# A recommendation tower on one core: one-hots compared against row numbers in PSUM, eight picked tables, strips in single runs, another order on PE, and filler products

## What is computed

```python
e = jnp.stack([tbl_f[ids[:, f]] for f in range(26)], axis=1)     # 512 x 26 x 128
sd = jnp.einsum('bfd,bd->bf', e, dense)
ss = jnp.einsum('bfd,bgd->bfg', e, e)
z = jnp.concatenate([dense, sd, ss[:, iu, ju]], axis=1)           # iu, ju: the pairs above the diagonal
h = jnp.concatenate([z, dense], axis=1)                           # 512 x 607
h = jnp.maximum(h @ W_top1 + b_top1, 0.0)                         # 512
h = jnp.maximum(h @ W_top2 + b_top2, 0.0)                         # 256
y = h @ W_top3                                                    # 512 x 1
```

## Time and profile before

| | |
|---|---|
| median of three runs | 146.29 us |
| the profiled execution | 145.72 us, of which the span (first to last instruction) 143.9 us |
| PE busy | 108.4 us (75%) |
| DVE busy | 65.0 us (45%) |
| ACT busy | 61.4 us (43%) |
| POOL busy | 82.6 us (57%) |
| DMA | 14.86 MB, 8258 packets, 4629 of them under 512 bytes |

### The profile page before, as it was taken

The page is one execution under the profiler, slowest core; times in us unless marked ns, Lnnn a source line. Parts: engine busy times, 40 slices in busy tenths (PEclk is TensorE's granted clock), DMA queues, the critical chain, the costliest instruction groups (busy, mean ns, idle before and its releaser), DMA issues.

```text
span 143.9 us, 1888 instructions
## 1 busy us (share of the span) xinstructions
PE 108.4 (75%) x692; PEld 97.4 (68%) x692; DVE 65.0 (45%) x138; ACT 61.4 (43%) x101; POOL 82.6 (57%) x76
## 2 busy tenths in 40 slices
PE   0007999999999999859509999979950989960792
PEld 0006778887887879758409997879940979950782
DVE  3079759999999934242400544215430013320011
ACT  4205077758997949818401245643320112320011
POOL 4788878998889977777777777777710000000000
PEclk9999999999999999999955999999997579996599
DMA  4999926999893342222232222321121000002000
GB/s 83 338 248 273 305 54 175 315 280 268 223 255 105 91 114 59 55 55 50 66 85 55 59 55 66 85 70 44 50 53 38 0 5 0 0 1 44 10 0 1
DMA packets 8258, 14.86 MB, mean 103 GB/s; under 512 B 4629, under 2 KB 4629, under 8 KB 8250
## 3 DMA queue, kind: packets, MB, share of 16 engines
q1 hardware_dynamic: 5805, 10.21, 25.5%
q0 software_dynamic: 2176, 4.46, 12.3%
q10 hardware_dynamic: 269, 0.09, 0.3%
HBM read 13.96 MB, written 0.00 MB: 97 GB/s over the span
## 4 chain that ended last, share of the span: by engine, by line
POOL 33%; PE 28%; SPq 13%; DMA 10%; issue 9%; DVE 3%; ACTq 2%; ACT 0%
POOL rows L289 33%; SPq L227 13%; PE ps_h_bank L368 12%; PE ps_gram L347 11%; DMA dots<-hot_ids 3%; DMA dots<-table 3%; ACTq L686 2%; DMA rows<-in_tbl,ids_sb 2%; PE ps_h_bank L388 1%; PE ps_dve L330 1%; DMA ids_sb<-in_ids 1%; DVE table L532 1%; DVE hot_ids L532 1%; PE ps_act L330 1%; PE ps_h_bank L400 1%
## 5 line engine op out<-in xcount | busy, mean ns | idle before, releaser
L289 POOL DMA_INDIRECT rows<-in_tbl,ids_sb x68 | 81.8, 1202 | 21.7 <-issue 20.4
L347 PE MATMUL ps_gram<-vecs 128*128 128x108 f32 x256 | 30.7, 276 | 1.1 <-issue 0.9
L498 DVE TENSOR_SCALAR one_hot<-hot_ids,row_id 125x512 fp32r<-125x512 int32 x67 | 27.9, 491 | 7.8 <-DMA hot_ids<-in_hot_ids 6.0
L302 PE MATMUL ps_gram<-one_hot,table_hi 125*128 125x512 f32 x78 | 31.2, 419 | 0.0
L347 PEld LDWEIGHTS ps_gram<-vecs 128*128 128x128 f32 x256 | 29.6, 192 | 1.9 <-issue 1.9
L302 PE MATMUL ps_gram<-one_hot,table_lo 125*128 125x512 f32 x78 | 30.6, 412 | 0.0
L368 PE MATMUL ps_h_bank<-dots,w_dots 128*128 128x128 f32 x96 | 17.6, 359 | 16.8 <-DMA dots<-hot_ids 10.0
L368 PEld LDWEIGHTS ps_h_bank<-dots,w_dots 128*128 128x128 f32 x96 | 16.4, 267 | 17.5 <-DMA dots<-table 7.2
L302 PEld LDWEIGHTS ps_gram<-one_hot,table_lo 125*128 125x128 f32 x78 | 15.5, 199 | 3.9
L302 PEld LDWEIGHTS ps_gram<-one_hot,table_hi 125*128 125x128 f32 x78 | 15.2, 200 | 3.4
L489 DVE COPY vecs<-ps_dve 128x512 f32<-128x512 f32 (+1 forms) x10 | 9.2, 923 | 14.9 <-PE ps_dve L330 14.9
(11 more groups left out here) (36 smaller groups left out, 83.6 us busy)
## 6 DMA issues: line engine op xcount, KB each, us to landing
table<-in_tbl SPq DMA_DIRECT2D x6, 448.0 KB
hot_ids<-in_hot_ids SPq DMA_DIRECT2D x3, 768.0 KB, 5.1
table<-in_tbl SPq DMA_DIRECT2D x3, 560.0 KB
rows<-in_tbl,ids_sb POOLq DMA_INDIRECT x68, 2.6
w_dots<-in_w_dots SPq DMA_DIRECT2D x3, 256.0 KB, 3.5
w_dense<-in_w_dense SPq DMA_DIRECT2D x2, 256.0 KB, 5.8
w<-in_W_top SPq DMA_DIRECT2D x2, 256.0 KB, 2.9
table<-in_tbl SPq DMA_DIRECT2D x6, 52.0 KB
```

The costliest lines, as they stand in the source:

```text
L289: pool.indirect_dma_start(out=rows[:, t % ROW_SETS, k, :], out_offset=None, in_=ins[f"tbl_{f}"], in_offset=bass.IndirectOffsetOnAxis(ap=id ...
L302: return pe.matmul(ps_pick[:, i % 2, :], part[0:KP, i % PART_RING, k, :], one_hot[0:KP, i % HOT_RING, k, :], start=(part is table_hi and k ...
L347: last = pe.matmul(ps_gram[:, part % 2 * BANKS + g // PER_BANK, c0:c0 + COLS], vecs[:, t % 2, p0:p0 + QUADS, :], vecs[:, t % 2, p0:p0 + QU ...
L498: nc.vector.tensor_scalar(one_hot[0:KP, i % HOT_RING, k, :], hot_ids[0:KP, i, :], row_id[0:KP, at + k:at + k + 1], None, ALU.is_equal).the ...
```

## The change

- `HOT` loses table 8 (1250 rows); eight tables are picked, 18 are gathered (72 gathers; the last batch of a tile has two tables).
- The row numbers are copied once to PSUM (`ps_row_id`). DVE makes the one-hots of two steps in one `tensor_tensor` of 125x1024, ids from SBUF and row numbers from PSUM, both read with step 0 along one dimension. ACT makes the last two steps of every table, table 0 included. DVE makes 6 of 8, or 8 of 10.
- ids are loaded as one table's, three and four tables' (`IDS_GROUPS`); the biases and `W_top3` are loaded later.
- `sums` is laid out so that each row's part of a strip is one run of 1536 bytes, and `gram` puts its four blocks of a bank 128 columns apart instead of 108.
- `fill(n)` on PE multiplies `ident` by itself into `ps_act`, n times; nobody reads the result. There are 18 such products before the first pick and 20 between `gram(3, 3)` and `layer_1_act(3)`.
- PE's, DVE's and ACT's lists are written in another order: the dense transposes come after `pick(0)`; layer 1 of a tile comes behind all four grams of the next tile (for tile 1 behind tile 0's layers, before `gram(2, 0)`).

The core of the diff:

```diff
-HOT_ROWS = {5: 1000, 6: 1000, 7: 1000, 16: 1000, 19: 1000, 24: 1000, 2: 1250, 3: 1250, 8: 1250}
+HOT_ROWS = {5: 1000, 6: 1000, 7: 1000, 16: 1000, 19: 1000, 24: 1000, 2: 1250, 3: 1250}
-KS_ACT = [[] if i == 0 else [KTS[i] - 1] if KTS[i] == 8 else [KTS[i] - 2, KTS[i] - 1] for i in range(NHOT)]
-KS_DVE = [[k for k in range(KTS[i]) if k not in KS_ACT[i]] for i in range(NHOT)]
+KS_ACT = [[KTS[i] - 2, KTS[i] - 1] for i in range(NHOT)]
+RUNS_DVE = [[(k, k + 2) for k in range(0, KTS[i] - 2, 2)] for i in range(NHOT)]
+IDS_GROUPS = [(0, 1), (1, 4), (4, NHOT)]
...
-                    "a (s b g) -> a s b g", s=QUADS, b=SLOTS)
+                    "a (q s j g) -> a q s j g", q=STRIPS, s=QUADS, j=STEPS)
...
+        ps_row_id = ps_h_bank[:, 1, H1 // 2 + P:H1 // 2 + P + sum(STEP_COUNTS)]
...
-            return (dots[STRIP_AT[q]:STRIP_AT[q] + n, t].rearrange("p s j g -> p s (j g)"),
-                    sums[t % 2][0:n, :, STEPS * q:STEPS * (q + 1), :].rearrange("a s j g -> a s (j g)"))
+            return (dots[STRIP_AT[q]:STRIP_AT[q] + n, t].rearrange("p s j g -> p (s j g)"),
+                    sums[t % 2][0:n, q].rearrange("a s j g -> a (s j g)"))
...
-                    c0 = g % PER_BANK * COLS
+                    c0 = g % PER_BANK * P
...
+            def fill(n):
+                for _ in range(n):
+                    pe.matmul(ps_act[:, 0, :], ident[:, :], ident[:, :], start=True, stop=True)
+
             pe.wait_ge(s_ident, 1)
+            fill(18)
             pick(0)
+            dense_transposes()
             pick(1)
...
             gram(3, 3)
-            layer_1_dense(3)
+            fill(20)
             layer_1_act(3)
...
-                for k in ks:
-                    nc.vector.tensor_scalar(one_hot[0:KP, i % HOT_RING, k, :], hot_ids[0:KP, i, :],
-                                            row_id[0:KP, at + k:at + k + 1], None, ALU.is_equal).then_inc(s_hot_dve, 1)
+                nc.vector.tensor_tensor(
+                    one_hot[0:KP, i % HOT_RING, k0:k1, :], hot_ids[0:KP, i, :].unsqueeze(1).to_broadcast(shape),
+                    ps_row_id[0:KP, at + k0:at + k1].unsqueeze(2).to_broadcast(shape), ALU.is_equal
+                    ).then_inc(s_hot_dve, 1)
```

More of the change, by code:

```diff
@@ L99, in build @@
         sums = [x[0:SLOTS].rearrange(order)[:, 0:QUADS * SLOTS * LANES].bitcast(F32).rearrange(
-                    "a (s b g) -> a s b g", s=QUADS, b=SLOTS)
-                for x, order in ((hot_ids, "a i n -> a (i n)"), (table, "a r k d -> a (r k d)"))]
+                    "a (q s j g) -> a q s j g", q=STRIPS, s=QUADS, j=STEPS)
+                for x, order in ((hot_ids_all, "a n -> a n"), (table, "a r k d -> a (r k d)"))]
         ps_dve = ps("ps_dve", [P, 4, P])
@@ L112, in build @@
         ps_pick = ps_gram[:, 2:4, :]
+        ps_row_id = ps_h_bank[:, 1, H1 // 2 + P:H1 // 2 + P + sum(STEP_COUNTS)]
         s_ids = sem("s_ids")
         s_dense = sem("s_dense")
-        s_hot_ids = [sem(f"s_hot_ids{n}") for n in range(NHOT // IDS_GROUP)]
+        s_hot_ids = [sem(f"s_hot_ids{n}") for n in range(len(IDS_GROUPS))]
         s_table = [sem(f"s_table{i}") for i in range(NHOT)]
@@ L401, in layer_3, with dense_transposes @@
                 last.then_inc(s_y, 1)
+            def dense_transposes():
+                pe.wait_ge(s_ident, 1)
+                pe.wait_ge(s_dense, 16)
+                for t in range(TILES):
+                    last = pe.transpose(ps_dve[:, t, :], dense[:, t, :], ident[:, :])
+                last.then_inc(s_dense_tp, 1)
+            def fill(n):
+                for _ in range(n):
+                    pe.matmul(ps_act[:, 0, :], ident[:, :], ident[:, :], start=True, stop=True)
             pe.wait_ge(s_ident, 1)
-            pe.wait_ge(s_dense, 16)
-            for t in range(TILES):
-                last = pe.transpose(ps_dve[:, t, :], dense[:, t, :], ident[:, :])
-            last.then_inc(s_dense_tp, 1)
+            fill(18)
             pick(0)
+            dense_transposes()
             pick(1)
+            transposes(0, 0)
             pick(2)
-            transposes(0, 0)
             transposes(0, 1)
@@ L415, in _ @@
             pick(4)
-            pick(5)
             transposes(0, 3)
             transposes(0, 4)
+            pick(5)
+            transposes(1, 0)
             pick(6)
+            transposes(1, 1)
             pick(7)
-            transposes(1, 0)
-            pick(8)
-            transposes(1, 1)
+            transposes(1, 2)
             pe.wait_ge(s_pad, 2)
             gram(0, 0)
+            transposes(1, 3)
             gram(0, 1)
-            transposes(1, 2)
             gram(0, 2)
-            transposes(1, 3)
+            transposes(1, 4)
             gram(0, 3)
-            transposes(1, 4)
             layer_1_dense(0)
@@ L507, in _ @@
             for i in range(NHOT):
-                one_hots(i, KS_DVE[i][0:2])
+                one_hots(i, 0)
                 low_part(i)
-                one_hots(i, KS_DVE[i][2:])
+                for n in range(1, len(RUNS_DVE[i])):
+                    one_hots(i, n)
                 if i == 1:
```

133 lines of the change are left out of this document (70 added, 63 removed).

## The result

The changed kernel takes 139.81 us (median of four runs, 138.10 to 140.51) beside 146.50 for the kernel before in the same session: ratio 0.951, 95% interval 0.940 to 0.963. It is faster by 4.9%, and 8.8 us slower than forecast, outside the range. Run again later beside other kernels (`changed_again`) it took 139.34 (ratio 0.956, 0.945 to 0.968). Some executions of a kernel are one to five per cent slower than its others: ratios leave those out, medians don't, and the traces of `no_first_fill`, `strips_four_runs` and `late_layers_sbuf` are of such an execution.

The account below looks back on a forecast made before the run. The prediction took the kernel as bound by PE's picks, then gathered rows, then a loop of strips, layer 1 and grams. Its steps reached a span of 128.8 us, plus 1.8 outside and 0.6 for the median: 131.0; range 126 to 138.

Parts of the forecast that it names:

- POOL: Gathers: held only by low parts, 5.2 us, not by new one-hots; last start 96.7 instead of 104.0.
- the rival priced held gathers at 10 us: New one-hots hold gathers as the old do: last gather starts at 109, `gram(3, 0)` +10, time 141; chance 0.11.
- the one-hots: In the picks: DVE's new two-step one-hots take 1.16 each, upper bound 2.10, and DVE is the bound.
- the ids at 6.6 and 12.7: Start of the picks: the first table's ids arrive at 6.6, the next ids at 12.7, at 316 KB/us.
- a new strip at 0.45: Strips on SP's queue: each takes 0.45 to issue instead of 0.79, upper bound 0.8.
- a rival at 136: Strips stay at 0.8: tile 2's strips +3.1, the last ones +1.6, time 136; chance 0.14.
- the clock: PE idles 4.6 us at tile 2's strips, then that tile's layer 1 runs at half rate and costs 5.5.
- the fillers: On PE: the first 18 products cost nothing; the last 20 end at 120.0, under cover of the last strips.
- The saving of a whole table is thus nearly eaten by the slower one-hots: In the picks: with one table fewer, `gram(0, 0)` at 53.0, only a little over a microsecond sooner than before.
- the order as what shortens the end: Behind the picks: PE is the bound from 53.0 to 92.8, and `gram(3, 0)` comes at 107.5 against 117.63.
- a slow start: At the start: part of a mild mixture with one-hots of 1.3; chance 0.04.
- the clock only as a gain: Layer 1 of tile 2 at full rate: 2.8 less, time 128; chance 0.08 together with other gains.

Follow-up runs that it names:

- no_first_fill: The changed kernel without the 18 filler products before the first pick: 139.85 us, ratio 0.947.
- strips_four_runs: The changed kernel with `sums` laid out as before, each row of a strip in four pieces again: 141.94 us, ratio 0.962.
- late_layers_sbuf: The order of `late_layers`, with DVE's one-hots from SBUF only, one instruction for each step: 136.07 us, ratio 0.943.
- one_hots_sbuf: The changed kernel with DVE's one-hots made as before, from SBUF only, one instruction for each step: 138.86 us, ratio 0.935.
- no_last_fill: The changed kernel without the 20 filler products before the last layer 1: 141.39 us, ratio 0.958.
- tile2_two_queues: The changed kernel with the third tile's strips shared between SP's queue (five) and ACT's (four): 135.44 us, ratio 0.924.
- ids_threes: The changed kernel with ids loaded in groups of three, three and two tables: 140.92 us, ratio 0.958.
- strip_forms: The changed kernel with 21 more DMAs on SP's queue behind the output, seven forms of strip, three each: 163.28 us, a time that means nothing.
- nine_tables: The changed kernel with the ninth table (1250 rows) picked as before, 17 gathered: 145.02 us, ratio 1.013.
- late_layers_relu: `late_layers` with ACT doing the relu of tile 2's layer 1 before issuing its share of the last strips: 127.10 us, ratio 0.875.
- late_layers: The changed kernel with the last tile's four grams ahead of tile 2's layers 1, 2 and 3, no last filler: 128.64 us, ratio 0.897.

## Why the prediction was wrong

The steps of the forecast against the trace after:

| | forecast | measured | added |
|---|---|---|---|
| `gram(0, 0)` | 53.0 | 55.4 | +2.4 |
| sums of tile 2 read | 91.7 | 95.9 | +1.8 |
| layer 1 of tile 2 begins | 97.4 | 104.1 | +2.5 |
| `gram(3, 0)` | 107.5 | 113.0 | -1.2 |
| last grams end | 115.5 | 122.8 | +1.8 |
| layer 1 of tile 3 begins | 120.6 | 129.3 | +1.4 |
| span | 128.8 | 137.7 | +0.2 |

- **Right: POOL.** Last gather at 95.6 (forecast 96.7). Seven gathers are lengthened by low parts, 3.7 together (forecast 5.2), and one, by 0.26, by another instruction with two SBUF inputs (`w_fold`, 52.60). The Trainium skill (SBUF — State Buffer, "SBUF: two separate sides") has DVE lock GpSimd out of the port pair in a two-port mode or with two SBUF inputs. The gathers of 0.94 beside the new one-hots, which have one input in PSUM, and the lengthened ones beside low parts agree. Its worth was wrong: the rival priced held gathers at 10 us, and `one_hots_sbuf`, where they are held in part (last start 99.2), is no slower.
- **Right: the one-hots.** 1.14 from start to start, forecast 1.16, and 1.22 for one alone; DVE has the picks' pace, as said: with cheaper one-hots they end 2.8 sooner.
- **Wrong: the ids at 6.6 and 12.7.** They came at 8.3 and 15.2. The rate of 316 KB/us came from one arrival of the profile of before, which two kernels with three tables' ids first missed by 2.3 to 2.6. DVE, being the bound, handed it all on: +2.4.
- **Wrong: a new strip at 0.45, "of the table load's form".** It costs 0.73. I took the number of pieces a row for what set the price and the table load, from HBM, for the nearest row; the source was what differed. It is the largest term: the wait of 1.28 at tile 0 (in the second line of the table), the +2.5 of the third and about 1 of the last strips' 1.4, 4.8 together of the 8.8. It was named as a rival at 136, 5 more than forecast; the rows of before held nothing that could exclude it, and 0.14 was too low.
- **Half right: the clock.** Layer 1 of tile 2 at half rate was foreseen, 5.5, and took 4.4 (4.4 to 5.5 in the profiles with this wait). That `gram(3, 0)` and the dense share then run partly at the lower clock, +1.8, was not. The two go together: where layer 1 took 5.05 to 5.49 (`no_last_fill`, `tile2_two_queues`, `ids_threes`, `strip_forms`) that gram took 2.01, where it took 4.37 to 4.88 the gram took 2.4 to 2.9 (but for `nine_tables`, 4.71 and 2.01). So the -1.2 and most of the +1.8 are one cost in two places.
- **Right: the fillers.** The first is worth nothing; the last, which the forecast gave no price, 1.6 by the medians, and it ended 1.9 before the strips, under cover.
- **Wrong: "The saving of a whole table is thus nearly eaten by the slower one-hots", and the order as what shortens the end.** `gram(0, 0)` did begin no sooner than in the profile of before (55.40 and 54.35), but that one had the early arrival. In the picks the table gives 4.7 (60.12 with nine) and the slower one-hots take 2.8 of it back (52.60 without them); in the whole time the table gives 4.5 to 5.2, and neither slower one-hots nor the order show a difference. Freeing the loop moved the wait from tiles 0 and 1 to tile 2, where the strips stand in single file with layer 1 and the grams behind it.

So three sizes failed on one side together: an arrival, a price and a clock. The range had dear strips (136) and a slow start as cases of their own, the clock only as a gain, and their sum in none. The last line of the sum is also 0.2 short: 128.8, 1.8 and 0.6 make 131.2, not 131.0.

## What to carry to other kernels

Before costing an edit at the start, ask whether the arrival from which its rate comes is itself typical; one profile can't say. Price a DMA's issue by a row with the same source and target memory, not the same shape. And when waits are moved from one place to another, look at what stands behind the last of them: here the last tile's grams needed nothing of the layers ahead of them, and putting them first was worth 11 to 12 us, more than the whole change (6.7).

## What the hardware showed unexpectedly

- A DMA from SBUF to SBUF takes 0.55 to 0.82 to issue on SP's queue, one from HBM to SBUF 0.29 to 0.43; from SBUF, 11 rows take 2.41 for three, 128 rows 1.83.
- The first strip on ACT's queue takes 1.49, the next ones 0.8. It is the first DMA of all on that queue: in `tile2_two_queues`, where ACT issues four strips twice, they take 3.90 and then 3.11.
- The first loads scatter: one load of ids arrived from 7.74 to 9.31, the second from 13.98 to 16.73 in kernels that load alike. The second, 768 KB, takes 11.4 from issue to landing beside tables and gathers (3.83 to 15.22).
- Ahead of the last layer 1 PE waited 0.26, 1.07 and 0.34 in `late_layers_relu` and 2.76, 0.55 and 0.34 in `late_layers`; the layer took 4.47 and 2.84. A step that starts sooner can come at the lower clock and end no sooner.
- The same filler and the same wait of 1.86 gave that layer 2.94 in the changed kernel (granted clock 1.00) and 4.24 in `ids_threes` (0.67).
